# A two-layer graph network on one core: node rows halved in two parts, dense scans in layer 1, float32r type products

## The reference

```python
# layer 0: 90 relations, each a mixture of 30 bases
W_rel = (w_comp @ V).reshape(90, 16, 16)
e     = concat([h[src] @ Ws.T, he @ Ws.T, h[dst] @ Ws.T]) @ Wa.T
h_out = segment_sum(einsum('ei,eio->eo', h[src], W_rel[rel_type]) * e, dst)
x     = layernorm(x + h_out)
# layer 1: 8 edge types, then a gated recurrent unit
A     = edge_emb[edge_type].reshape(-1, 16, 16)
m     = segment_sum(einsum('emh,eh->em', A, x[src]), dst)
gi, gh = m @ w_ih.T + b_ih, x @ w_hh.T + b_hh
r, z  = sigmoid(i_r + h_r), sigmoid(i_z + h_z)
n     = tanh(i_n + r * h_n)
x     = layernorm(x + (1 - z) * n + z * x)
```

## Time and profile before

| | |
|---|---|
| time, median of 3 runs | 5613.58 us (5613.08 to 5614.38) |
| the profiled execution's own time | 5610.07 us |
| its span | 5608.2 us |
| TensorE clock granted, mean | 0.943 |
| busy, PE / PEld | 4950.1 (88%) / 4647.6 (83%) us |
| busy, DVE / ACT / POOL | 4712.6 (84%) / 4374.3 (78%) / 4055.1 (72%) us |
| chain that ended last | DVE 45%, PE 30%, issue 13%, DMA 5%, POOL 3% |
| PE's look-ups and products, layer 0 / layer 1 | 275.75 to 2803.3 / 2978.24 to 5434.65 us |

### The profile page before, as it was taken

How to read it: one execution, slowest core, us unless ns; L and a number is a source line. 1 busy time by engine, 2 the same in 40 slices (tenths; PEclk the granted TensorE clock), 3 DMA queues, 4 the chain that set the end, 5 groups by cost and what they waited for, 6 DMA issues and landing times.

```text
span 5608.2 us, 106498 instructions
## 1 busy us (share of the span) xinstructions
PE 4950.1 (88%) x36141; PEld 4647.6 (83%) x36141; DVE 4712.6 (84%) x7893; ACT 4374.3 (78%) x5373; POOL 4055.1 (72%) x4261
## 2 busy tenths in 40 slices
PE   4597999999999999999948998999899899989974
PEld 1297999999999999999937888888888888888863
DVE  6589999999999999999936888888888888888864
ACT  5686888888888888888727888888888888888864
POOL 3376777777777777777766777777777777777766
PEclk8698999999999999999958999999999999999985
DMA  9811111111111111111121222222221122222221
GB/s 302 333 29 33 37 39 39 33 40 40 40 40 40 39 40 40 36 39 38 31 71 23 18 18 17 17 17 18 17 17 16 16 17 17 17 17 17 17 21 12
DMA packets 628151, 239.45 MB, mean 43 GB/s; under 512 B 520872, under 2 KB 601467, under 8 KB 627448
## 3 DMA queue, kind: packets, MB, share of 16 engines
q10 hardware_dynamic: 421742, 84.19, 8.6%
q0 software_dynamic: 136160, 39.20, 8.5%
q1 hardware_dynamic: 70186, 115.26, 6.0%
HBM read 72.97 MB, written 164.99 MB: 42 GB/s over the span
## 4 chain that ended last, share of the span: by engine, by line
DVE 45%; PE 30%; issue 13%; DMA 5%; POOL 3%; DVEq 1%; ACT 1%; ACTq 0%; SPq 0%; POOLq 0%
PE ps_table L717 26%; DVE work L1239 10%; DVE t_buf L1231 10%; DVE scanned L1197 9%; DVE t_buf L1243 8%; POOL sums L549 2%; DMA rows<-type_table,idx 2%; DVE rows L1246 2%; PE ps_table L727 1%; PE ps_misc L699 1%; DMA relation_table<-scanned 1%; DVE he_dot L1297 1%; DVE he_dot L1283 1%; POOL rows L549 1%; DMA relation_table<-t_buf 1%
## 5 line engine op out<-in xcount | busy, mean ns | idle before, releaser
L717 PE MATMUL ps_table<-node_halves,hot_key 128*128 128x320 f32 x24960 | 3910.1, 315 | 322.5 <-DVE t_buf L1231 307.8
L717 PEld LDWEIGHTS ps_table<-node_halves,hot_key 128*128 128x128 f32 x24960 | 3727.3, 191 | 389.3 <-DVE t_buf L1231 354.2
L888 ACT ACTIVATE hot_key<-ps_misc,less_key 128x512 fp32r<-128x512 f16 x3120 | 1874.7, 694 | 900.3 <-PE ps_misc L699 892.1
L549 POOL DMA_INDIRECT rows<-relation_table,idx x1976 | 1898.0, 961 | 660.7 <-issue 500.5
L549 POOL DMA_INDIRECT rows<-type_table,idx x1976 | 1866.7, 945 | 629.0 <-issue 515.5
L892 ACT ACTIVATE hot_key<-hot_key,ones 128x2560 fp32r<-128x2560 f32 x624 | 1520.5, 2437 | 20.3
L1231 DVE TENSOR_TENSOR t_buf<-ps_table,work 128x640 f32<-128x640 f32 x1248 | 1007.7, 811 | 199.3 <-PE ps_table L717 199.1
L1239 DVE TENSOR_REDUCE work<-t_buf 128x64 f32<-128x1280 f32 x624 | 927.3, 1486 | 21.4
L1243 DVE TENSOR_TENSOR t_buf<-ps_table,work 128x1024 f32<-128x1024 f32 x624 | 763.8, 1224 | 82.2 <-DVE work L1239 21.4
L1246 DVE TENSOR_REDUCE rows<-t_buf 128x64 f32<-128x1024 f32 x624 | 761.7, 1221 | 21.4
L727 PE MATMUL ps_table<-rel_mats,hot_type 90*128 90x256 bf16 x3744 | 463.8, 274 | 0.0
(11 more groups left out here) (206 smaller groups left out, 1624.8 us busy)
## 6 DMA issues: line engine op xcount, KB each, us to landing
scanned<-scanned ACTq DMA_DIRECT2D x52, 992.0 KB, 3.9
relation_table<-scanned SPq DMA_DIRECT2D x50, 765.0 KB, 6.6
relation_table<-t_buf SPq DMA_DIRECT2D x48, 765.0 KB, 6.6
rows<-relation_table,idx POOLq DMA_INDIRECT x1976
rows<-type_table,idx POOLq DMA_INDIRECT x1976
scanned<-scanned ACTq DMA_DIRECT2D x52, 496.0 KB
he<-in_edge_attr SPq DMA_DIRECT2D x48, 496.0 KB
type_table<-t_buf SPq DMA_DIRECT2D x14, 448.0 KB, 3.0
```

Of the source, the lines that this page charges most:

```text
L549: pool.indirect_dma_start(out=rows[:, k, :], out_offset=None, in_=table, in_offset=bass.IndirectOffsetOnAxis(ap=index[:, k:k + 1], axis=0) ...
L717: last = pe.matmul(ps_banks[:, duo * DUO + t, 0:BLOCK_W], hot_key[:, b, g, edges], node_halves[:, half, g, :, :].rearrange("p f j -> p (f ...
L888: act.activation(hot_key[:, b, g, :], match_bank[:, 0, :], ACT.Abs, bias=less_key[:, g:g + 1])
```

## The change

It has three parts.

1. The type matrices are kept as float32r halves, like the nodes: `rel_mats` has 2 halves for 3 bf16 parts, `type_mats` 2 strips for 3, and `hot_type` is float32r too. The one helper `halve` takes the place of `halve_nodes`' body and of `split` here. One small DMA of `emb_sb` falls away (`LATE_IN` 14 to 13).
2. The nodes for layer 1 are halved in two parts. The first 16 of 20 columns of each block (`EARLY`, all that the first 12 groups fill) are done ahead of the last pair of groups, behind a new wait for `state_set` at 12. The other 4 are done right behind the last group, ahead of the waits for the stores.
3. In layer 1 the scans write to `scanned1`, a dense view of the same buffer (62 x 16 per partition and half, no gaps), and ACT's store of it is dense on both sides.

```diff
-        rel_mats = sb("rel_mats", [RELS, 3, D, D], BF16)
-        emb_sb = sb("emb_sb", [3 * STRIP, D * D])
-        type_mats = sb("type_mats", [3 * STRIP, D * D], BF16)
+        rel_mats = sb("rel_mats", [RELS, 2, D, D], F32R)
+        emb_sb = sb("emb_sb", [2 * STRIP, D * D])
+        type_mats = sb("type_mats", [2 * STRIP, D * D], F32R)
...
-        hot_type = sb("hot_type", [P, 2, QUAD * P], BF16)
+        hot_type = sb("hot_type", [P, 2, QUAD * P], F32R)
...
+        scanned1 = scanned[:, :, :, :].rearrange("p h c f -> p h (c f)")[:, :, 0:CHUNK * D].rearrange(
+            "p h (c f) -> p h c f", f=D)
...
-                  [rel_mats[:, k, :, :].rearrange("r o i -> r (o i)") for k in range(3)], rows0),
-            Layer(1, types_sb, TYPES, 3 * STRIP, [type_mats[:, :]], rows1),
+                  [rel_mats[:, k, :, :].rearrange("r o i -> r (o i)") for k in range(2)], rows0),
+            Layer(1, types_sb, TYPES, 2 * STRIP, [type_mats[:, :]], rows1),
...
-                        act.dma_start(stored[:, col(i * 2 + h), :], scanned[:, h, :, 0:stored.shape[2]]
-                                      ).then_inc(scan_out[h], 16)
+                        act.dma_start(stored[:, col(i * 2 + h), :], kept[:, h, :, :]).then_inc(scan_out[h], 16)
...
+            def halve(value, top, halves):
+
+                step(dve.tensor_scalar(top.bitcast(I32), value.bitcast(I32), -(1 << 12), None, ALU.bitwise_and))
+                step(dve.tensor_copy(halves[0], top))
+                return dve.tensor_tensor(halves[1], value, top, ALU.subtract)
+
+            def halve_nodes(nodes, lo=0, hi=BLOCK_TILES):
+                return halve(nodes.rearrange("p (j g) f -> p g f j", g=BLOCKS)[:, :, :, lo:hi],
+                             whole[:, 0:PADDED * D].rearrange("p (g f j) -> p g f j", g=BLOCKS, f=D)[:, :, :, lo:hi],
+                             [node_halves[:, k, :, :, lo:hi] for k in range(2)])
...
-                return dve.tensor_tensor_scan(scanned[:, h, :, at + f], cont, messages[:, :, f],
-                                              scanned[:, 1 - h, CHUNK - 1, at + f:at + f + 1], ALU.mult, ALU.add)
+                return dve.tensor_tensor_scan(kept[:, h, :, at + f], cont, messages[:, :, f],
+                                              kept[:, 1 - h, CHUNK - 1, at + f:at + f + 1], ALU.mult, ALU.add)
...
-            type_parts = [whole[0:3 * STRIP, k * D * D // 2:(k + 1) * D * D // 2].bitcast(BF16) for k in range(3)]
-            step(split(emb_sb[:, :], by_in[0:3 * STRIP, 0, :, :].rearrange("p o i -> p (o i)"), type_parts))
-            for k in range(3):
-                own = slice(k * STRIP, (k + 1) * STRIP)
-                last = dve.tensor_copy(type_mats[own, :], type_parts[k][own, :])
-            last.then_inc(product_mats_set[1], 1)
+            type_top = whole[0:2 * STRIP, 0:D * D]
+            step(dve.tensor_scalar(type_top.bitcast(I32), emb_sb[:, :].bitcast(I32), -(1 << 12), None,
+                                   ALU.bitwise_and))
+            dve.tensor_copy(type_mats[0:STRIP, :], type_top[0:STRIP, :])
+            dve.tensor_tensor(type_mats[STRIP:2 * STRIP, :], emb_sb[STRIP:2 * STRIP, :],
+                              type_top[STRIP:2 * STRIP, :], ALU.subtract).then_inc(product_mats_set[1], 1)
...
-            pair(0)
-            with dve.Fori(1, GROUPS // 2) as i:
-                pair(i)
-
+            EARLY = (GROUPS - 2) * GROUP // BLOCKS
+            pair(0)
+            with dve.Fori(1, GROUPS // 2 - 1) as i:
+                pair(i)
+            dve.wait_ge(state_set, GROUPS - 2)
+            step(halve_nodes(state[:, :, :], 0, EARLY))
+            pair(GROUPS // 2 - 1)
+            dve.wait_ge(state_set, GROUPS)
+            halve_nodes(state[:, :, :], EARLY, BLOCK_TILES).then_inc(node_parts_set, 1)
+            dve.wait_ge(node_parts_set, 1)
...
                 dve.wait_ge(scan0_out[h], 16 * PAIRS)
                 dve.wait_ge(t1_out[h], 16 * (GROUPS // 2))
-            dve.wait_ge(state_set, GROUPS)
             dve.wait_ge(yT_sb, GROUPS)
-            halve_nodes(state[:, :, :]).then_inc(node_parts_set, 1)
-            dve.wait_ge(node_parts_set, 1)
...
-                                last_scan = scan(h, 0, f, rows1[:, h, :, :])
+                                last_scan = scan(scanned1, h, 0, f, rows1[:, h, :, :])
```

More of the change, by code:

```diff
@@ L432, in _ @@
             with nc.allow_non_contiguous_dma(reason="small weights, transposed once"):
-                for k in range(3):
+                for k in range(2):
                     sp.dma_start(emb_sb[k * STRIP:k * STRIP + TYPES, :], edge_emb).then_inc(late_in, 16)
@@ L892, in one_hot, with chunks_out @@
                 act.activation(hot_key[:, b, :, :], hot_key[:, b, :, :].bitcast(F32), ACT.Relu, bias=ones[:, 0:1], scale=-1.0)
-                act.activation(types, types, ACT.Relu, bias=ones[own, 0:1], scale=-1.0).then_inc(match_set[lay.n], 1)
-            def chunks_out(lay, stored, scan_set, scan_out):
+                act.activation(types, types.bitcast(F32), ACT.Relu, bias=ones[own, 0:1], scale=-1.0
+                               ).then_inc(match_set[lay.n], 1)
+            def chunks_out(lay, stored, kept, scan_set, scan_out):
                 for q in range(1, lay.quads):
@@ L917, in _ @@
             one_hot(layers[0], 0, 0, 0)
-            chunks_out(layers[0], scan0_v, scan0_set, scan0_out)
+            chunks_out(layers[0], scan0_v, scanned, scan0_set, scan0_out)
             one_hot(layers[1], 0, 0, 0)
@@ L939, in _ @@
                 pair(i)
-            chunks_out(layers[1], scan1_v, scan1_set, scan1_out)
+            chunks_out(layers[1], scan1_v, scanned1, scan1_set, scan1_out)
             def rows_out(g):
@@ L1124, in relation_parts @@
                 dve.wait_ge(rel_parts_set, 1)
-                split(rel_rows[:, :, :].rearrange("r i o -> r o i"),
+                halve(rel_rows[:, :, :].rearrange("r i o -> r o i"),
                       whole[0:RELS, 0:D * D].rearrange("r (o i) -> r o i", i=D),
-                      [rel_mats[:, k, :, :] for k in range(3)]).then_inc(product_mats_set[0], 1)
+                      [rel_mats[:, k, :, :] for k in range(2)]).then_inc(product_mats_set[0], 1)
                 dve.wait_ge(product_mats_set[0], 1)
```

27 lines of the change are left out of this document (8 added, 19 removed).

## The result

| | before | after |
|---|---|---|
| median of 11 runs | 5612.91 us | 5599.32 us |
| lowest and highest | 5610.52 and 5614.87 | 5596.35 and 5600.81 |
| the profiled execution's own time, its span | 5610.07, 5608.2 | 5599.62, 5596.9 |

The ratio is 0.9975 (95% interval 0.9966 to 0.9984): 13.6 us less. The forecast was 11.8 us less and 5601.8 us. In a second comparison the changed kernel took 5596.27 against 5609.39 us, 13.1 us less (0.9976, 0.9966 to 0.9986).

The account below looks back on a forecast made before the run. Layer 0 was taken as bound by DVE and layer 1 by POOL, so only the first chunk (-0.7), the passage (-6.8) and the end (-4.3) count: -11.8 us, from 5613.58 to 5601.8 us, range 5597.5 to 5608.

Parts of the forecast that it names:

- What bounds each stage: Layers 0 and 1: layer 0 bound by DVE (96.7% busy), layer 1 by POOL, where DVE waits 4.6 us per chunk.
- The first chunk of layer 0: Where PE is awaited: five products before the last look-ups, 0.15 us less each, 0.7 us less in all.
- the price of a float32r product: Products on PE: 0.148 us each, taken from the float32r look-up, so eight take 1.18 us against 1.33 for twelve bf16.
- The low bound of the prediction: Products of layer 0: a float32r product at the bf16 step, 0.11 us, would save 0.44 us per group.
- Layer 1's products: Four float32r for four bf16: PE gets 0.15 us more per group, 0.9 us per chunk, with no effect on the time.
- the cover: Layer 1: the 4.6 us per chunk that DVE waits for gathered rows hides PE's extra work; without it 47 us.
- The passage: Between the layers: PE begins 8.8 us sooner, held gathers cost 2.0 us, sum -6.8 us, between -5 and -9.
- The 2.0 us for the held gathers: Passage, beside the early halving: one gather caught in the subtraction makes the one behind it 2.0 us later; bounds 1.3 and 3.2.
- the reading of the gather of 80.82: It outlasted the first halving instruction and ended inside the next two, so a gather gets in during the cast (copy).
- Rival 1: Passage: the cast holds POOL too, one gather waits through all three instructions, 3.2 us late; -10.6, 5603.0 us; chance 0.18.
- The end: Last store of layer 1: dense, it lands in 3.0 us in place of 7.30, 4.3 us less, between 3.4 and 4.6.
- Sum: Whole kernel: -0.7 - 6.8 - 4.3 = -11.8 us, median 5601.8 us; forecast's chance 0.50.

## Why the prediction was right

**What bounds each stage: right.** Layer 1 goes by POOL. Doubling the products left its steady period as it was, tripling them moved the period to what six quads of PE take. The prediction had read this from the wait of 4.6 us per chunk for rows, against the chain of waits that puts most of the layer on PE; PE's free 4.6 us (47.45 less six quads of 7.15) is the same size. Layer 0 stayed at 48.1 us with four products fewer per quad, as it must if DVE sets it.

**The first chunk of layer 0: right in kind, too small.** The step that failed is the price of a float32r product, 0.148 us taken from the look-up. It is 0.117, and the look-up's longer step goes with its 320 moving columns. Five quads by 0.38 us are 1.9 us in place of 0.7, and the traces of layer 0 show 1.6 to 2.7. The low bound of the prediction (0.11) was nearer.

**Layer 1's products: the cover was right, the price was not.** A quad is 0.31 us longer, not 0.15 (7.14 against 6.83 when PE waits for nobody). The step that failed is that the price was taken from the middle of a row of like matmuls. The cost stands at the changes from one kind to the next: the first product starts 0.24 us behind the last look-up (0.15 with bf16), the second 0.22 behind the first (0.12), the next transpose 0.21 behind the last product (0.11). The cover of 4.6 us hides six quads, 1.9 us. Only in the first chunk, where POOL follows the look-ups closely, 0.3 us came through.

**The passage: right in its sum, wrong in how the gathers are held.** 8.8 us sooner was forecast; from the last gather of sums PE's begin came 9.1 us sooner and the first gather 9.4. The halved nodes stand at 2962.44 (forecast 2964), and t1_sb is late next. The 2.0 us for the held gathers came out as 2.0, but not as told, so that the agreement of this term is luck. One gather was to be held by the subtraction alone; there were three, by 0.62, 0.31 and 1.05 us. The step that failed is the reading of the gather of 80.82, that a gather gets in during the copy. The row of the copy that follows that cut, in the kernel before, says otherwise:

```profile
82.11 0.99 DVE L1016 CAST node_halves<-whole 128x1600 fp32r<-128x1600 f32 x1
```

The copy ends at 83.10 and the gather at 83.22, 0.12 us behind it, just as the gather of 2941.28 ended 0.12 us behind its cut. Had it got in between the cut and the copy, it would have ended 0.8 us behind the cut, at 82.88; the copy held it once more. Rival 1, that one gather would be held through all three instructions, failed as well: the gather of 2943.15 ended 0.82 us behind the copy, in the middle of the subtraction, which did not hold it. Why a gather under way is held by the cut and the copy and not by the subtraction stays open. The rule of the Trainium skill beside that rival ("SBUF — State Buffer", SBUF: two separate sides) has the copy right; it speaks of a lock for one instruction, and the trace agrees with that: the cost was 2.0 us and not the 3.2 that the rival made of three instructions in a row. It also gives the lock to whichever of the two starts first, and there the trace differs: the gather of 2941.28 began 0.21 us ahead of the cut and was the one held.

Over more traces the passage spreads: from the last gather of layer 0 to the first of layer 1 it takes 173.7 to 174.8 us in the three profiles with the halving in one piece behind the waits, and 166.1 to 167.8 in the seven with the halving in two parts, 7.1 us less in the mean, where 6.8 was forecast.

**The end: right.** 4.3 us forecast, 4.7 to 4.8 in the traces. The dense store of 496 KB landed in 2.6 us, less than the 3.0 of the 448 KB in the table's pieces.

**Sum.** -1.9 + 0.3 - 7.4 (-9.4 + 2.0) - 4.7 is -13.7 us, beside 13.6 by the medians; -11.8 was forecast, and most of the difference is the product's price. That the two agree to 0.1 us is chance, since the passage alone spreads by more than 1 us between traces. What the prediction didn't see is that the time could be had without the 2.0 us: it checked that the early part had room on DVE, and never asked whether the late place had room for all of it. It had: 5.4 us of halving, and 6.7 us from its begin to the end of the table copy.

## What to carry to other kernels

When a step is moved ahead of a wait, ask first whether the whole of it fits between its inputs and the next thing that is late; here the split cost 2 us that one move would not have. What an engine may be given to do in a loop is the loop's period less what the engine needs when it waits for nobody. Here 2.8 us more in a chunk stayed inside it and left the pace alone, and of 5.6 us more the 1.0 that passed it came through. A price taken from another shape has to be scaled by what sets it, and what a change from one shape to the next costs is a term of its own.

## What the runs showed of the hardware

- A gather of POOL that starts inside a long copy or subtraction of DVE is held and ends 0.8 us behind it: 1.26 us with a start inside the copy, 2.00 inside the subtraction, against 0.95. The cut and the copy also hold one that is under way, which then ends 0.12 us behind them (1.57 and 1.60 us with the cut begun 0.21 and 0.24 us behind the gather's start; the copy and the gather of 80.82). A subtraction that began behind the gather did not hold it.
- Float32r products with 128 weight columns start 0.117 us apart at 2.4 GHz, with 256 moving columns as with 256 and 128 in turn; bf16 ones with 256 start 0.109 apart. At 320 moving columns the float32r look-ups start 0.147 apart. A change from look-ups to the products of layer 1 and on to transposes cost 0.3 us per quad more in float32r than in bf16.
- A store of 496 KB to HBM landed in 7.3 to 7.4 us when its source lay in pieces of 64 B, and in 2.6 us from one dense piece per partition.
- The mean gather differed by 2 ns (944 to 946) between executions of the same or like kernels, spread over all its places. Over the 1976 gathers of layer 1 that is 3 to 4 us, as much as one part of this change moved, so a difference of two profiles was no measure of a part by itself.
- With PE busier in layer 1 its granted clock was higher: in the stretch of 474.4 us it was 0.97 before (PE busy for 430.9 us), 0.98 after (443.7) and 1.00 with doubled products (463.4).
